# Attention softmax and null value handled another way, and the scores moved back in each TensorE slot

## The chip, the cores and the metric

The kernel runs on one core of one Trainium2 chip. Its time is the device time of one execution in microseconds (us). TensorE (PE in the profile), VectorE (DVE), ScalarE (ACT) and GpSimd (POOL) each work through their own list of instructions in order, SyncE (SP) issues most of the transfers, and the lists meet only at semaphores.

## The reference

Four layers are added to x in turn, x of shape 2 x 1024 x 256. Two are causal attention with 16 heads of 64 and one key and value that all heads share; two are mixtures of 8 experts of width 128 (best two of eight, plus a shared expert of width 256). Cut to what the change touches, for each of the two attention layers:

```python
xn = ln(x, g)
q = heads(xn @ Wq)                       # 16 heads of 64 (first layer: l2-normalised, scaled)
k, v = split(xn @ Wkv)                   # one k and one v of 64 for all heads
k = concat([null_kv[0], k]); v = concat([null_kv[1], v])     # a null key and value ahead
sim = q @ k.T * scale + concat([null_bias, bias])
sim = where(causal & mask, sim, -inf)
out = softmax(sim) @ v                   # the null column has a weight too
y = ln(out.reshape(b, n, 16 * 64) @ Wout, g_out)
x = x + y
```

So the output of a head is (sum over keys of p times v, plus p_null times v_null) divided by (sum of p, plus p_null).

## The kernel before

All operands of the large matmuls are split into a float16 high part and a float16 low part, and `three` (lines 1084 to 1088) adds high x high, high x low and low x high in PSUM. After a head of some 90 us (position bias table, weights) come the two attention layers and then the two expert layers.

**Steps, units, slots.** Attention is cut into 512 steps. Step n is one head of one 128-row tile of one batch item. Four heads (h = n % 4) make a unit, 8 units (4 head groups x 2 items) are one tile T, and there are 8 tiles a layer. With causality tile t (0 to 7) has nk = t + 1 key blocks of 128 columns, so a step is 128 to 1024 columns wide. This text calls the eight tiles of the first layer T0 to T7 and those of the second T8 to T15 (as wide as T0 to T7). Every engine runs the same loop over slots n, with m, k = divmod(n, 4), and does in slot n what is due for several steps at different distances:

- PE: the scores of step n + 3 (L1203, L1204), then by k the projection by Wo (k = 0, L1214 to L1219), the projection of q of unit m + 3 (k = 1), the transposes of q (k = 3, L1227); then the transposes of the probabilities of step n into `tp` (L1312), the products of step n - 1 with v (`pv`, L1152) and the small things of `small()` (at k = 2 the transposes of the normalised output, L1300).
- DVE: score plus bias and its row maximum for step n + 2 (L880), at k = 3 the low part of q (L908), then the low part of the probabilities `p_lo` (L964), and small things.
- ACT: exp of step n + 1 (L630), at k = 3 the high part of q (`q_b`, L651, and its copy into `q_a`, L655), then the high part of the probabilities `p_hi` (L722).
- POOL: null column, normalisation, the splitting of the weights.

**Groups.** The probabilities are transposed block by block into one of two PSUM banks `tp`, copied to `p_hi` and subtracted to `p_lo` by groups of up to four blocks of one head. A step of 1 to 4 blocks is one group, one of 5 to 8 blocks is two. Buffers: two `tp`, four `p_hi`, four `p_lo`, two `probs`, two `biased`, two score banks `sc`, one bank `op` for the four heads of a unit. PSUM bank `aux` serves everything else, one user after the other (`take`); in tiles of at most four key blocks the unused half of a score bank helps out (`free_banks`).

**Row sums, null column, output.** The exp (L630) also writes the sum of its row (`accum_out`, `rows`). At k = 3 POOL forms `d_null` (L506), ACT `p_null` (L731), POOL `denom` (L511) and `o_null` = p_null x v_null for the four heads (L514). At k = 1 of the next unit DVE adds `op` and `o_null` into `o_raw` (L859), which frees `op` for the next unit, and takes the reciprocal (L862); POOL multiplies into `o_n` (L479), PE transposes, ACT and DVE split, and PE projects by Wo at k = 0.

## Time and profile before

| what | value |
|---|---|
| median of 3 runs | 1735.9 us (1734.8 to 1736.44) |
| the profiled execution | 1732.54 us |
| span of its instructions | 1730.6 us |
| mean granted TensorE clock | 0.972 |
| attention, from the first to the last start of L880 | 89.58 to 1353.2 us |
| busy share of the span | PE 85%, DVE 81%, ACT 70%, POOL 43% |

The span runs from the first to the last instruction; the profiled execution's own time has some 2 us around it. Busy time of an engine in a stretch is the time in which at least one of its instructions was under way, and an idle time is put down to what released it.

### The profile page before, as it was taken

The numbers are of one execution on the slowest core, as the hardware profiler recorded it, in microseconds if no ns is written. First come the engines' busy times: TensorE is split into PE (matmuls) and PEld (weight loads), VectorE is DVE, ScalarE is ACT, GpSimd is POOL, SyncE is SP. The second block draws the span as 40 slices with busy tenths as digits, with TensorE's granted clock in tenths as the row PEclk, the third lists the DMA queues.
The fourth block names the chain that finished last, engine by engine and source line by source line (L and its number), as shares of the span: only waits on it lengthen the run. The fifth ranks groups of instructions, "written<-read, shape, count | busy, mean of one in ns | idle before, by whom it ended". The sixth has DMA issues, their size and how long they took to land.

```text
span 1730.6 us, 46424 instructions
## 1 busy us (share of the span) xinstructions
PE 1470.3 (85%) x16377; PEld 1081.0 (62%) x16377; DVE 1410.4 (81%) x3651; ACT 1210.2 (70%) x3064; POOL 751.0 (43%) x1412
## 2 busy tenths in 40 slices
PE   2467778888889999977888888999999799999998
PEld 1245556666677777766666666777777555555555
DVE  4557778888889999977788888999999687777777
ACT  1268778888889899978888888989999432332232
POOL 5557776443434334366554232223222365522222
PEclk9779999999999999989999999999999899999999
DMA  4002122111211223012121212221223000000000
GB/s 138 7 24 62 51 62 75 57 62 69 75 58 67 87 99 99 33 44 62 51 81 52 85 63 75 75 81 62 82 99 99 1 25 19 1 1 1 13 13 25
DMA packets 50440, 96.70 MB, mean 56 GB/s; under 512 B 3332, under 2 KB 27028, under 8 KB 50212
## 3 DMA queue, kind: packets, MB, share of 16 engines
q1 hardware_dynamic: 45504, 90.27, 15.8%
q10 hardware_dynamic: 4708, 3.45, 0.7%
q8 instruction: 135, 2.21, 0.5%
q14 instruction: 93, 0.76, 0.1%
HBM read 91.54 MB, written 2.17 MB: 54 GB/s over the span
## 4 chain that ended last, share of the span: by engine, by line
PE 42%; DVE 21%; ACT 14%; issue 11%; POOL 3%; DMA 1%; DVEq 0%; ACTq 0%; SPq 0%; POOLq 0%
PE tp L1312 7%; DVE p_lo L964 7%; ACT p_hi L722 6%; DVE biased L880 5%; PE sc L1203 3%; PE sc L1086 3%; PE sc L1087 3%; PE sc L1088 3%; ACT q_b L651 3%; PE sc L1204 3%; ACT probs L630 3%; PE op L1086 2%; PE aux L1086 2%; PE tp L1086 2%; PE aux L1088 2%
## 5 line engine op out<-in xcount | busy, mean ns | idle before, releaser
L964 DVE TENSOR_TENSOR p_lo<-tp,p_hi 128x512 f16<-128x512 f32 (+3 forms) x768 | 416.6, 554 | 121.3 <-ACT p_hi L722 114.3
L880 DVE CUSTOM_DVE_ANT_0 biased<-sc,bias,neg_null 128x256 f32<-128x256 f32 (+7 forms) x512 | 411.0, 803 | 2.7 <-issue 0.8
L630 ACT ACTIVATE probs<-biased,neg_max 128x256 f32<-128x256 f32 (+7 forms) x512 | 395.7, 773 | 14.2 <-DVE neg_max L880 12.7
L1312 PE MATMUL tp<-ident,probs 128*128 128x128 f32 x2304 | 388.7, 278 | 17.7 <-DVE p_lo L964 15.5
L722 ACT ACTIVATE p_hi<-tp 128x512 f16<-128x512 f32 (+3 forms) x768 | 368.9, 491 | 43.6 <-PE tp L1312 33.5
L1086 PE MATMUL op<-v_s,p_hi 128*128 128x64 f16 x2304 | 284.9, 194 | 54.4 <-DVE p_lo L964 35.9
L1203 PE MATMUL sc<-k_a,q_a 128*128 128x512 f16 (+3 forms) x768 | 254.2, 331 | 66.2 <-DVE neg_max L880 59.3
L1312 PEld LDWEIGHTS tp<-ident,probs 128*128 128x128 f32 x2304 | 267.9, 142 | 52.9 <-issue 37.9
L1088 PE MATMUL op<-v_s,p_lo 128*128 128x64 f16 x2304 | 284.0, 194 | 0.0
L1087 PE MATMUL op<-v_s,p_hi 128*128 128x64 f16 x2304 | 283.9, 194 | 0.0
L1086 PEld LDWEIGHTS op<-v_s,p_hi 128*128 128x128 f16 x2304 | 216.0, 99 | 85.5 <-DVE p_lo L964 62.1
L1204 PE MATMUL sc<-k_b,q_b 128*128 128x512 f16 (+3 forms) x768 | 241.9, 329 | 0.0
L1087 PEld LDWEIGHTS op<-v_s,p_hi 128*128 128x128 f16 x2304 | 210.3, 98 | 7.5
L1088 PEld LDWEIGHTS op<-v_s,p_lo 128*128 128x128 f16 x2304 | 210.5, 98 | 0.0
L570 POOL TENSOR_TENSOR p_lo<-probs,p_hi 128x512 f16<-128x512 f32 x80 | 92.5, 1156 | 213.7 <-ACT p_hi L755 213.3
L511 POOL TENSOR_TENSOR denom<-rows,p_null 128x4 f32<-128x4 f32 x128 | 25.6, 200 | 324.9 <-ACT p_null L731 324.9
L1203 PEld LDWEIGHTS sc<-k_a,q_a 128*128 128x128 f16 x768 | 75.1, 98 | 129.5 <-DVE neg_max L880 88.5
L755 ACT ACTIVATE p_hi<-probs 128x512 f16<-128x512 f32 x80 | 50.4, 630 | 145.5 <-DVE probs L1068 145.5
L479 POOL TENSOR_TENSOR o_n<-o_raw,r_den 128x256 f32<-128x256 f32 x128 | 78.4, 613 | 146.7 <-DVE o_raw L859 145.7
L908 DVE TENSOR_TENSOR q_a<-aux,q_b 64x256 f16<-64x256 f32 x256 | 108.1, 422 | 27.6 <-ACT q_b L651 19.9
L1063 DVE SCALAR_TENSOR_TENSOR biased<-sc,biased 128x512 f32<-128x512 f32 x80 | 55.2, 689 | 69.2 <-ACT biased L751 69.2
L651 ACT ACTIVATE q_b<-aux 64x256 f16<-64x256 f32 x256 | 96.5, 377 | 20.4 <-PE aux L1227 14.4
(257 smaller groups left out, 3611.4 us busy)
## 6 DMA issues: line engine op xcount, KB each, us to landing
bias<-rel_table SPq DMA_DIRECT2D x4, 2048.0 KB, 8.5
bias<-in_fside_16xSxS SPq DMA_DIRECT2D x4, 2048.0 KB, 7.9
bias<-rel_table SPq DMA_DIRECT2D x4, 1792.0 KB, 7.9
bias<-in_fside_16xSxS SPq DMA_DIRECT2D x4, 1792.0 KB, 7.1
bias<-rel_table SPq DMA_DIRECT2D x4, 1536.0 KB, 7.3
bias<-in_fside_16xSxS SPq DMA_DIRECT2D x4, 1536.0 KB, 6.7
bias<-rel_table SPq DMA_DIRECT2D x4, 1280.0 KB, 5.6
bias<-in_fside_16xSxS SPq DMA_DIRECT2D x4, 1280.0 KB, 6.3
```

The lines of the kernel that those rows point to most:

```text
L630: ac.activation(probs[:, i % 2, 0:w], biased[:, i % 2, 0:w], ACT.Exp, bias=neg_max[:, u % 2, i % HU:i % HU + 1], scale=-1.0, accum_out=row ...
L651: ac.activation(heads(q_b[0:DH, u % 2, :], e), first[e * DH:(e + 1) * DH, 0:UW].rearrange("p (c q) -> p c q", q=P), ACT.Copy)\
L722: ac.activation(p_hi[:, gi % 4, 0:nb * P], tp[gi % 2][:, 0:nb * P], ACT.Copy)\
L880: ve.tensor_tensor_reduce(out=biased[:, i % 2, 0:w], in0=sc[i % 2][:, 0:w], in1=bias[:, g % 2, i % HU, 0:w], scale=-1.0, scalar=neg_null[: ...
L908: ve.tensor_tensor(heads(q_a[DH:P, u % 2, :], e), first[e * DH:(e + 1) * DH, 0:UW].rearrange("p (c q) -> p c q", q=P), heads(q_b[0:DH, u % ...
L964: ve.tensor_tensor(p_lo[:, gi % 4, 0:nb * P], tp[gi % 2][:, 0:nb * P], p_hi[:, gi % 4, 0:nb * P], ALU.subtract).then_inc(s["p_lo"], 1)
L1086: te.matmul(out_, l_hi, r_hi, start=first, stop=False)
L1087: te.matmul(out_, l_hi, r_lo, start=False, stop=False)
L1088: return te.matmul(out_, l_lo, r_hi, start=False, stop=last)
L1203: te.matmul(o_, q_a[:, u % 2, cols], k_a[layer][:, bt, c0:c0 + cw], start=True, stop=False)
L1204: last = te.matmul(o_, q_b[:, u % 2, cols], k_b[layer][:, bt, c0:c0 + cw], start=False, stop=True)
L1312: last = te.transpose(tp[gi % 2][:, jj * P:(jj + 1) * P], probs[:, n % 2, (j0 + jj) * P:(j0 + jj + 1) * P], ident[:, :])
```

## The change

1. **Ones column.** `v_s` gets a 65th column, 1 in the high part and 0 in the low part, so that the product with v gives the row sum in `op` too (65 columns a head). The exp loses `accum_out`, and `rows` goes.
2. **Groups across heads.** The blocks of the four heads of a unit are counted through, and four in a row make a group, whatever head they are of. Each group is full. `p_hi` and `p_lo` are made when a group is complete, in the slot of the head that completes it.
3. **q copy on DVE.** The copy of `q_b` into `q_a` (64 x 512 float16, SBUF to SBUF) goes from ACT to DVE, ahead of the two L908.
4. **Null value at the projection.** `o_null`, `o_raw` and POOL's `o_n` go. DVE adds `p_null` to the row sums in `op`, takes the reciprocal and multiplies `op` by it into `o_n`. POOL keeps p_null / denom in `pn` (at k = 2), PE transposes `pn` once all 16 heads of a tile and item are there (k = 3), ACT copies it to `pn_t`, and the projection by Wo gets one more float32 matmul, `pn_t` x `nv_w`, for the last head group. `nv_w` = v_null x Wo per head is made once a layer (slot 12) by 24 matmuls.
5. **Order.** In each PE slot the scores of step n + 3 stand behind the first part of the transposes of step n, and so also behind the projections and the transposes of q.
6. Around it: a few memsets and copies in the head, `wt_n`, `wg_n`, `cond_n` inside `bias`, the load of the second bias waits for their use, `d_null` at k = 2, `p_null` doubled.

```diff
@@ class Plan
+        for u in range(self.steps // HU):
+            nk = self.tile(u * HU) + 1
+            blocks = [(u * HU + h, j) for h in range(HU) for j in range(nk)]
+            for b0 in range(0, len(blocks), 4):
+                group = blocks[b0:b0 + 4]
...
+                self.finished[group[-1][0]].append(len(self.groups))
+                self.groups.append(group)
@@ POOL
-                if k == 1 and 1 <= m <= NU:
+                if k == 2 and 1 <= m <= NU:
                     u = m - 1
-                    pool.wait_ge(s["o_raw"], u + 1)
...
-                    gp.tensor_tensor(o_n[:, :, :], o_raw[:, :, :],
-                                     r_den[:, :].unsqueeze(2).to_broadcast([P, HU, DH]), ALU.mult)\
-                        .then_inc(s["o_n"], 1)
...
+                    gp.tensor_tensor(pn[:, T % 2, bt, hg * HU:(hg + 1) * HU], p_null[:, u % 2, :], r_den[:, :], ALU.mult)\
+                        .then_inc(s["pn"], 1)
...
-                    gp.tensor_tensor(denom[:, :], rows[:, u % 2, :], p_null[:, :], ALU.add).then_inc(s["denom"], 1)
...
-                    gp.tensor_tensor(o_null[:, :, :], null_v[:, :].unsqueeze(1).to_broadcast([P, HU, DH]),
-                                     p_null[:, :].unsqueeze(2).to_broadcast([P, HU, DH]), ALU.mult)\
-                        .then_inc(s["o_null"], 1)
@@ ACT
                     ac.activation(probs[:, i % 2, 0:w], biased[:, i % 2, 0:w], ACT.Exp,
-                                  bias=neg_max[:, u % 2, i % HU:i % HU + 1], scale=-1.0,
-                                  accum_out=rows[:, u % 2, i % HU:i % HU + 1]).then_inc(s["probs"], 1)
+                                  bias=neg_max[:, u % 2, i % HU:i % HU + 1], scale=-1.0).then_inc(s["probs"], 1)
...
-                    act.wait_ge(s["q_hi"], 2 * (u + 1))
-                    ac.activation(q_a[0:DH, u % 2, :], q_b[0:DH, u % 2, :], ACT.Copy).then_inc(s["q_dup"], 1)
...
+                    if k == 3 and 0 <= m - 1 < NU and (m - 1) % UNITS >= UNITS - B:
...
+                        ac.activation(pn_t[:, u % B, :], turned(pn_ps) if u < U0 else pn_ps, ACT.Copy)\
+                            .then_inc(s["pn_s"], 1)
...
-                        act.wait_ge(s["pt"], gi + 1)
+                        act.wait_ge(s["pt"], plan.group_end[gi])
...
+                        ac.activation(p_hi[:, gi % 4, :], tp[gi % 2][:, :], ACT.Copy).then_inc(s["p_hi"], 1)
@@ DVE
-                    dve.wait_ge(s["o_null"], u + 1)
+                    dve.wait_ge(s["p_null"], u + 1)
                     dve.wait_ge(s["pv"], plan.groups_done(n - 2))
-                    ve.tensor_tensor(o_raw[:, :, :], op[:, 0:UW].rearrange("p (h d) -> p h d", h=HU),
-                                     o_null[:, :, :], ALU.add).then_inc(s["o_raw"], 1)
-                    dve.wait_ge(s["denom"], u + 1)
+                    link(ve.tensor_tensor(denom[:, :], o_ps[:, :, DH], p_null[:, u % 2, :], ALU.add))
+                    if u >= 1:
+                        dve.wait_ge(s["pn"], u)
                     ve.reciprocal(r_den[:, :], denom[:, :]).then_inc(s["r_den"], 1)
+                    dve.wait_ge(s["r_den"], u + 1)
+                    if u >= 1:
+                        dve.wait_ge(s["ot"], u)
+                    ve.tensor_tensor(o_n[:, :, :], o_ps[:, :, 0:DH],
+                                     r_den[:, :].unsqueeze(2).to_broadcast([P, HU, DH]), ALU.mult).then_inc(s["o_n"], 1)
...
                     dve.wait_ge(s["q_hi"], 2 * (u + 1))
+                    ve.tensor_copy(q_a[0:DH, u % 2, :], q_b[0:DH, u % 2, :]).then_inc(s["q_dup"], 1)
@@ PE, pv
+                    last = three(op[:, h * (DH + 1):(h + 1) * (DH + 1)], p_hi[:, gi % 4, cols], p_lo[:, gi % 4, cols],
+                                 v_hi, v_lo, j == 0, j == nk - 1)
@@ PE, slot n (the scores stood here, ahead of everything)
-                i = n + 3
-                if 0 <= i < N:
...
-                    last.then_inc(s["scores"], 1)
                 if k == 0 and 0 <= m - 2 < NU:
...
+                    if hg == HG - 1:
+                        pe.wait_ge(s["pn_s"], u // UNITS * B + u % B + 1)
...
+                        last = te.matmul(first[:, 0:D], pn_t[:, u % B, :], nv_w[:, :], start=False, stop=True)
...
+                    if k == 3 and 0 <= m - 1 < NU and (m - 1) % UNITS >= UNITS - B:
+                        u = m - 1
+                        T, bt = u // UNITS, u % B
+                        take(True, (s["pn_s"], T * B + bt + 1))
+                        pe.wait_ge(s["pn"], u + 1)
+                        te.transpose(second[0:H, 0:P], pn[:, T % 2, bt, :], ident[:, :]).then_inc(s["pn_t"], 1)
...
+                for j in range(max(1, len(parts), len(before))):
+                    if j < len(parts):
                         pe.wait_ge(s["probs"], n + 1)
+                        for _, jb in parts[j]:
+                            gi, at_ = plan.group_of[n, jb]
+                            if at_ == 0 and gi >= 2:
+                                pe.wait_ge(s["p_lo"], gi - 1)
+                            last = te.transpose(tp[gi % 2][:, at_ * P:(at_ + 1) * P],
+                                                probs[:, n % 2, jb * P:(jb + 1) * P], ident[:, :])
+                            if at_ == 3 or jb == nk - 1:
+                                last.then_inc(s["pt"], 1)
+                    if j == 0 and 0 <= n + 3 < N:
+                        scores(n + 3)
                     if j < len(before):
                         pv(before[j])
                     if j == 0:
```

## Rows read from the trace of the kernel before

**Rows 1.** The page: busy us of each engine, share of the span, instructions.

```profile
PE 1470.3 (85%) x16377; PEld 1081.0 (62%) x16377; DVE 1410.4 (81%) x3651; ACT 1210.2 (70%) x3064; POOL 751.0 (43%) x1412
```

**Rows 2.** Stretch, us, busy us by engine: T0-T3, T4-T7, T8-T11, T12-T15; T7.

```profile
89.58:356.79 267.21, 201.43 (x2330) 152.33 (x2331) 204.09 (x669) 213.85 (x674) 170.55 (x340) 0.95 0.18 54
356.79:741.11 384.32, 352.60 (x4632) 272.96 (x4629) 349.62 (x801) 338.70 (x797) 157.69 (x310) 1.00 0.21 72
741.11:988.60 247.49, 202.65 (x2427) 157.94 (x2425) 197.12 (x640) 204.98 (x632) 132.11 (x281) 0.97 0.21 61
988.60:1353.20 364.60, 341.11 (x4552) 267.28 (x4551) 331.11 (x748) 324.83 (x741) 95.76 (x204) 1.00 0.22 79
...
638.43:741.11 102.68, 99.16 (x1348) 78.06 (x1347) 98.66 (x197) 93.63 (x194) 42.84 (x85) 1.00 0.22 75
```

**Rows 3.** Who waited for whom, whole span: total us, times, longest.

```profile
DVE p_lo L964 <- ACT p_hi L722: 114.3, 275, 2.0
...
DVE q_a L908 <- ACT q_b L651: 19.9, 44, 1.5
...
ACT p_hi L722 <- PE tp L1312: 33.5, 105, 0.6
...
PE sc L1203 <- DVE neg_max L880: 59.3, 119, 2.6
...
PE op L1086 <- DVE o_raw L859: 15.8, 16, 1.9
```

**Rows 4.** Groups by line and shape: count, busy us, mean ns, idle before.

```profile
L964 DVE TENSOR_TENSOR p_lo<-tp,p_hi 128x512 f16<-128x512 f32 x384 | 262.9, 689 | 70.1 <-ACT p_hi L722 66.1
...
L630 ACT ACTIVATION_READ_ACCUMULATOR probs<-biased,neg_max 128x1 f32 x512 | 100.3, 196 | 0.0
...
L655 ACT ACTIVATE q_a<-q_b 64x512 f16<-64x512 f16 x128 | 80.6, 630 | 4.0
...
L964 DVE TENSOR_TENSOR p_lo<-tp,p_hi 128x128 f16<-128x128 f32 x128 | 36.4, 285 | 17.4 <-ACT p_hi L722 16.0
...
L987 DVE BATCH_NORM_AGGREGATE y_mv<-y_st 128x2 f32<-128x6 f32 x32 | 5.8, 182 | 1.1
```

**Rows 5.** Timeline of ACT, then DVE, in T1: start us, length us.

```profile
151.27 0.39 ACT L722 ACTIVATE p_hi<-tp 128x256 f16<-128x256 f32 x1
151.53 0.52 ACT L630 ACTIVATE probs<-biased,neg_max 128x256 f32<-128x256 f32 x1
151.93 0.21 ACT L630 ACTIVATION_READ_ACCUMULATOR probs<-biased,neg_max 128x1 f32 x1
152.02 0.39 ACT L722 ACTIVATE p_hi<-tp 128x256 f16<-128x256 f32 x1
...
149.94 0.42 DVE L964 TENSOR_TENSOR p_lo<-tp,p_hi 128x256 f16<-128x256 f32 x1 [0.44 <-ACT p_hi L722]
150.28 0.15 DVE L947 SCALAR_TENSOR_TENSOR neg_null<-sc,null_b 128x4 f32<-128x4 f32 x1
```

**Rows 6.** Single lines: duration ns min/median/max.

```profile
L901 DVE TENSOR_SCALAR xn<-x,mv,rstd x32: 400/409/819, 59.7 to 1217.9; 128x256 f32<-128x256 f32 x32
...
L827 DVE COPY p_hi<-null_k x2: 180/180/181, 41.1 to 41.5; 128x64 f32<-128x64 f32 x2
...
L840 DVE COPY cond_t<-op x1: 140/140/140, 48.8 to 48.8; 64x2 f32<-64x2 f32 x1
...
L1105 PE MATMUL sc<-bias,moe_w x32: 379/379/793, 38.0 to 46.9; 128*128 128x256 f32 x32
```

**Rows 7.** Groups by line and shape: the same L901, with its mean.

```profile
L901 DVE TENSOR_SCALAR xn<-x,mv,rstd 128x256 f32<-128x256 f32 x32 | 16.6, 557 | 8.5 <-POOL rstd L523 8.4
```

**Rows 8.** Timeline of T7, of PE: start us, length us, how many (x).

```profile
685.79 0.27 PE L1086 MATMUL aux<-wq,moe_w 128*128 128x256 f16 x1
...
686.45 0.60 PE L1312 MATMUL tp<-ident,probs 128*128 128x128 f32 x4
...
686.88 0.19 PE L1086 MATMUL op<-v_s,p_hi 128*128 128x64 f16 x1
...
```

More of the change, by code:

```diff
@@ L78, in unit @@
         return n // HU
-    def of(self, n):
-        return range(self.first_group[n], self.first_group[n + 1])
     def at(self, n):
-        return list(self.of(n)) if 0 <= n < self.steps else []
+        return self.finished[n] if 0 <= n < self.steps else []
     def groups_done(self, n):
-        return self.first_group[n + 1]
+        return max((gi for i in range(n // HU * HU, n + 1) for gi in self.finished[i]), default=-1) + 1
 def model(nc, a, out):
@@ L257, in model @@
                     x_st x_rs xn xt xt_hi xt_lo xr_hi xr_lo kv kv_act kv_r kv_d kv_v k_dup kt k_hi k_lo
-                    d_null p_null denom r_den o_null o_raw o_n ot ot_hi ot_lo y y_s y_acc
+                    d_null p_null r_den pn pn_t pn_s nv_w nv_o o_n ot ot_hi ot_lo y y_s y_acc
                     y_st y_rs y_n x_new""")
@@ L386, in _ @@
             load_bias(sp, 0)
+            sp.wait_ge(setup["mt"], 1)
             load_bias(sp, 1)
@@ L422, in _ @@
             gp.memset(ones64[:, :], 1.0).then_inc(setup["ones"], 1)
+            gp.memset(nv_f, 0.0).then_inc(setup["nv0"], 1)
+            for i in range(2):
+                for hl in range(2):
+                    gp.memset(v_s[i][:, :, hl, DH:DH + 1], 1.0 - hl).then_inc(setup["v1"], 1)
             for e in range(E):
@@ L832, in _ @@
                              kn_a[0:DH, :], ALU.subtract).then_inc(setup["nkb"], 1)
+            dve.wait_ge(setup["nv0"], 1)
+            for e in range(2):
+                half = slice(e * DH, (e + 1) * DH)
+                last = ve.tensor_copy(nv_f[half, e::18], nv_c[half, 0:1].to_broadcast([DH, INNER // P]))
+            link(last)
+            nv_f3 = nv_f.rearrange("p (c h) -> p c h", h=H)
+            link(ve.tensor_copy(nv_s[:, 0, :, :], nv_f3))
+            ve.tensor_tensor(nv_s[:, 1, :, :], nv_f3, nv_s[:, 0, :, :], ALU.subtract).then_inc(setup["nvs"], 1)
             dve.wait_ge(setup["mt"], 1)
@@ new lines, in small @@
+                    if n in NULL_AT:
+                        layer = NULL_AT.index(n)
+                        take(True, (s["nv_o"], layer + 1))
+                        pe.wait_ge(setup["nvs"], 1)
+                        pe.wait_ge(job_done, job_end[3 * layer + 2])
+                        for c in range(INNER // P):
+                            last = three(second[0:H, 0:D], nv_s[:, 0, c, :], nv_s[:, 1, c, :],
+                                         wo[layer][:, 0, c, :], wo[layer][:, 1, c, :], c == 0, c == INNER // P - 1)
+                        last.then_inc(s["nv_w"], 1)
@@ new lines, in _, with scores @@
+                nk = plan.tile(n) + 1 if 0 <= n < N else 0
+                def scores(i):
+                    layer, t, u = plan.layer(i), plan.tile(i), plan.unit(i)
+                    bt, h = u % B, i % HU
+                    if i == 0:
+                        pe.wait_ge(setup["penalty"], 2)
+                        pe.wait_ge(setup["mm"], 3)
+                    if h == 0:
+                        pe.wait_ge(s["q_dup"], u + 1)
+                        pe.wait_ge(s["q_lo"], 2 * (u + 1))
+                        if u % UNITS == 0:
+                            pe.wait_ge(s["k_lo"], u // UNITS + 1)
+                    if i >= 2:
+                        pe.wait_ge(s["biased"], i - 1)
+                    cols = slice(h * P, (h + 1) * P)
+                    w = P * (t + 1)
+                    if w > 512:
+                        release(i % 2)
+                        free[i % 2] = ()
+                    for c0 in range(0, w, 512):
+                        cw = min(512, w - c0)
+                        o_ = sc[i % 2][:, c0:c0 + cw]
+                        te.matmul(o_, q_a[:, u % 2, cols], k_a[layer][:, bt, c0:c0 + cw], start=True, stop=False)
+                        last = te.matmul(o_, q_b[:, u % 2, cols], k_b[layer][:, bt, c0:c0 + cw],
+                                         start=False, stop=True)
+                    last.then_inc(s["scores"], 1)
```

175 lines of the change are left out of this document (81 added, 94 removed).

## The prediction, made blind

> **What bounds the kernel now.** I read the page first, then the busy time by stretch, then the list of waits, then the groups by shape, and the timeline last, for how instructions follow on one another. The page alone misleads: PE is busy 85%, DVE 81%, ACT 70% [rows 1], but that is a mean over a head, attention and the expert layers, and the change touches attention alone, 1263.6 us of the span. There no single engine is the bound. In the narrow tiles (T0 to T3, T8 to T11) DVE, ACT and PE are each busy 75 to 83% of the time, in the wide ones (T4 to T7, T12 to T15) 88 to 94%, and in T7 PE has 99.2, DVE 98.7 and ACT 93.6 of 102.7 us [rows 2]. PE's figure flatters it in narrow tiles, since matmuls overlap, but in T7 its issue is really full: a projection of six matmuls takes from 685.79 to 686.45, four transposes from there to 686.88, and the products follow at once [rows 8]. So a wide tile is set by DVE and PE together, and a narrow one by the handovers between three engines that work in order.
>
> I count in DVE's time, because DVE is in every handover and full in the wide tiles. Its busy time in attention is 204.1 + 349.6 + 197.1 + 331.1 = 1081.9 us, its idle time 181.7: 63.1, 34.7, 50.4 and 33.5 in the four stretches [rows 2]. Of this 114.3 us is `p_lo` waiting for `p_hi` on ACT, 19.9 is q's low part waiting for its high part; `p_hi` itself waited only 33.5 for the transposes, so mostly ACT was late because it was busy [rows 3].
>
> **The change, part by part, in DVE time.** One thing first. Lengths are not spacings. The read of the accumulator behind each exp is 0.196 us long [rows 4], but the next ACT instruction starts 0.09 after it; a 0.39 us copy is followed after 0.26; and on DVE a 0.42 us instruction after 0.34 [rows 5]. Back to back, ACT saves some 0.12 and DVE some 0.08 of each length. I take spacings.
>
> *ACT is relieved.* Ones column: 512 reads x 0.09 = 46 us (not the 100.3 that the group shows). The q copy: 128 x (0.63 - 0.12) = 65 [rows 4]. Groups: before, a unit of four heads has 4 groups up to four key blocks and 8 above, after it has nk. Over a layer that is 8 x (16 + 32) = 384 against 8 x 36 = 288, so 192 fewer over both layers, and the columns stay the same. A `p_hi` of 256 columns takes 0.26 of spacing, of which I put 0.05 down as fixed: 10 us. Together ACT loses 121 of its 1082 us in attention [rows 2, 5].
>
> *DVE is loaded.* `p_lo`: 285 ns for 128 columns and 689 for 512 give 135 ns per block and 150 fixed [rows 4], 0.07 in spacing; 192 x 0.07 = -14 us. `o_raw` becomes `o_n`, the same shape and also out of PSUM: nothing. `denom`: four columns, as L947's 0.15 us [rows 5], 0.07 in spacing. It and the reciprocal now each hand over to the next instruction of DVE itself, which loses the 0.08 overlap and the 0.03 that a chained L987 idles (1.1 us over 32) [rows 4]: 2 x 0.11. The q copy is an operation that the trace does not show at this size. Below: 0.14, a copy of 2 columns. Above: 0.69, the 128 x 512 subtraction. A copy of 64 float32 columns takes 0.18, so 0.65 ns a column [rows 6]; 512 at that rate are 0.47, and at twice the rate, as half the bytes, 0.30. I take 0.30, in spacing 0.22. To it I add 0.10 for hold-ups: L901, a one-input instruction from SBUF to SBUF as the copy is, has a median of 409 ns, a maximum of 819 and a mean of 557 [rows 6, 7]. So 0.32 + 0.07 + 0.22 = 0.61 us a unit, x 128 = +78. Net DVE work: +64 us, 16 in each stretch.
>
> The Trainium skill (VectorE: DVE Perf Modes, the errata section) prices such a copy at 58 + 512/4 cycles at 0.96 GHz, 0.19 us; by it the sum would be 14 us lower. No row here has a float16 copy out of SBUF that could confirm it.
>
> *The waits.* With ACT 11% lighter, `p_hi` comes sooner. In T0 to T2 and T8 to T10 it also comes less often (1 to 3 times a unit instead of 4). And the transposes no longer stand behind scores that wait for the row maximum of two steps before; PE idled 59.3 us there [rows 3]. The transposes are never later for it: before they stood behind everything that they stand behind now, and the scores too. The scores come later by the projections and transposes, at most some 1.7 us, but are wanted by DVE only in the next slot, and a slot is 2.1 us on average in T0 to T3 (267.2/128) and 3.2 in T7. So DVE's idle time should about halve: I take 32, 16, 28 and 16 us off the four stretches (little from T7, where only 4.0 is left), 92 of 181.7. With the added work that gives -16, 0, -12 and 0: **-28 us**. The wide tiles end about even because two effects cancel; T7 alone should be slower, by 1 to 5 us, and the narrowest tiles gain most.
>
> *PE is loaded.* 32 float32 matmuls of 256 columns at 0.38 [rows 6] are 12 us; 32 transposes at 0.11, 48 matmuls for `nv_w` at 0.11 (six of 256 columns in 0.66 us [rows 8]) and one column more in 6912 products (0.4 ns each, estimated from 0.11 us for 256) are 3.5, 5 and 3. Of these 24 us I count a quarter, 6: DVE is now the fuller engine in wide tiles and PE idles in narrow ones. If PE stayed the fuller one all 24 would show. The products of a unit's first group wait until `op` is read; that was one DVE instruction (15.8 us of PE idle [rows 3]) and is three, 0.6 us more, but transposes and scores now stand ahead of it, and in T0 to T2 its place moves on a slot or more. POOL loses 128 x two 256-column multiplies; it is at 43% [rows 1] and releases nobody on the path now: nothing. `d_null` comes a slot earlier, nothing. The head gets some five small DVE instructions at 0.15 to 0.2, partly in the way: +1. The expert layers: nothing.
>
> **Sum.** -28 + 6 + 1 = -21 us against the profiled execution's 1732.5, so 1711.5. That execution lies 3.4 below the median of the runs, so 1715 in their terms; I say 1714.
>
> **Rivals.** *A, the q copy is dear (slower).* Work on DVE is paid in full where DVE is full. The sum is zero when a unit costs DVE not 0.61 but 0.61 + 21/128 = 0.77 us, that is when the copy with its hold-ups takes 0.48 instead of 0.32. With 0.47 for the copy (no gain from float16) and half of L901's worst excess (0.41) on top it is 0.60: 128 x 0.28 = +36, **1750 us**. For it: the spread of L901. Against it: at k = 3 POOL has less to do than before. The Trainium skill (SBUF — State Buffer, Who interferes with whom) states a rule for this: a DVE copy from SBUF to SBUF that uses the second port pair and a POOL instruction exclude each other for their whole length. L901's 400 and 819 ns agree with it. 0.16.
>
> *B, the idle time nearly goes.* If lifting ACT and moving the transposes leaves DVE idle only 50 us (4% of the time, as T7 has now), the sum falls by 40: **1674 us**. For it: in narrow tiles all four slots of a unit have a wait for `p_hi` now and most lose it. Against it: the waits for PE on q, x and k stay. 0.16.
>
> *C, `aux` at k = 3.* In wide tiles the transpose of `pn` uses `aux` right after q's transposes, so PE must wait inside the slot until DVE has read q, ahead of its second part of transposes. 8 wide tiles x 2 units x about 1 us (copy and two L908, less what PE does meanwhile) = +16: **1730 us**. 0.12.
>
> *D, the order of waits is what holds it*, ACT was not: idle time falls by 50, not 92, work is added, +42: **1756 us**. Against it: the two waits on ACT are 134 of the 181.7. 0.08.
>
> **How the numbers follow.** My case has 0.48 and its own range is 1698 to 1730. With A to D the range reaches from B's 1674 to near A's 1750; cutting 1 in 10 at each side gives 1677 to 1745. About 0.2% (3.5 us) is what a measurement of this kernel can tell from no change, so faster is below 1732.4: my case nearly whole, B and two thirds of C, 0.72; within 0.2%, the top of my case and the rest of C, 0.09; slower, A, D and the tail of C, 0.19.
>
> **What would show it.** In the profile after: no accumulator reads on ACT, 576 `p_hi` and 576 `p_lo`, all of 512 columns; ACT's busy time in attention down by some 120; DVE's up by some 65 and its idle time near 90, with `p_lo` waiting for `p_hi` 114.3 down to about 45; T0 to T3 near 251 us and T8 to T11 near 235, T7 at 104 to 108. The copy's row decides A: 0.30 us with a mean under 0.4 is mine. I would be wrong if DVE in the wide tiles were held by PE after all (then all 24 us of PE's extras show), or if idle time in narrow tiles came from PE's in-order waits for `aux`, which the change does not lift.

## The result, and the profile after

The changed kernel takes 1847.8 us (median of 4 runs, 1846.9 to 1856.6) against 1736.2 for the kernel before beside it: ratio 1.065, interval 1.062 to 1.069. It is 112 us slower; 1714 was forecast. One of the four executions of e4 below had a granted clock of 0.65 and took 2216 us; it is left out of e4's times.

The page of the changed kernel: busy us of each engine.

```profile
PE 1512.1 (82%) x16521; PEld 1116.1 (60%) x16521; DVE 1474.3 (80%) x3719; ACT 1089.0 (59%) x2266; POOL 602.8 (33%) x1161
```

Against [rows 1] ACT has lost 121 us and POOL 148, DVE has gained 64 and PE 42. The busy times of ACT and DVE came out almost as forecast, and the time did not follow them. The same windows as in [rows 2], of the changed kernel (T0-T3, T4-T7, T8-T11, T12-T15, T7); the last columns are granted clock, DMA share and GB/s.

```profile
90.13:369.27 279.14, 210.10 (x2366) 157.22 (x2367) 218.71 (x685) 180.51 (x473) 135.23 (x278) 0.93 0.16 50
369.27:796.53 427.26, 365.18 (x4657) 287.65 (x4656) 367.59 (x817) 311.12 (x598) 119.99 (x247) 0.98 0.19 66
796.53:1060.23 263.70, 209.32 (x2474) 161.75 (x2472) 208.53 (x655) 174.01 (x432) 94.89 (x216) 0.94 0.20 56
1060.23:1465.00 404.77, 351.90 (x4579) 277.59 (x4576) 349.09 (x762) 296.09 (x543) 59.16 (x140) 1.00 0.20 71
680.78:796.53 115.75, 103.15 (x1363) 81.59 (x1362) 103.80 (x213) 86.57 (x157) 33.55 (x70) 1.00 0.20 66
```

Attention went from 1263.6 to 1374.9 us, and all four stretches are longer: by 11.9, 42.9, 16.2 and 40.2 us. DVE is busy 1143.9 us there (+62) and idle 231 (it was 181.7, and some 90 was forecast). In T7 no engine is full any more: of 115.8 us PE works 103.2, DVE 103.8, ACT 86.6. In the wide tiles every engine has become less full: the change made waits. PE's granted clock (the third number from the end) is a little lower too, 0.98 for 1.00 in T4 to T7 and 0.94 for 0.97 in T8 to T11; no run separates what that adds. Who waited for whom in the changed kernel:

```profile
PE op L1120 <- DVE p_lo L998: 82.0, 79, 2.3
...
DVE p_lo L998 <- ACT p_hi L743: 77.7, 134, 2.0
...
ACT probs L639 <- PE tp L1372: 68.2, 93, 1.7
ACT p_hi L743 <- PE tp L1372: 67.9, 136, 1.5
...
ACT probs L639 <- DVE neg_max L914: 56.3, 70, 1.6
...
PE aux L1238 <- DVE ot_lo L989: 38.2, 41, 1.5
...
DVE neg_null L982 <- PE sc L1302: 34.2, 42, 3.6
...
PE aux L1120 <- DVE q_a L943: 26.0, 44, 1.2
...
DVE denom L888 <- PE op L1122: 21.8, 42, 1.2
...
PE aux L1319 <- DVE q_a L943: 19.4, 16, 1.9
```

The waits have moved to PE. DVE's wait for ACT's `p_hi` fell by 37 us, from 114.3 [rows 3] to 77.7 (about 45 was forecast). But DVE now waits 56 us for PE, for the product of the null column (`neg_null`) and for the products with v (`denom`); before, the first was not there and the second, then `o_raw`'s, was under 1 us. ACT waits 136 us for PE's transposes of the probabilities (68.2 + 67.9, before 33.5 [rows 3]), and 56 for DVE's row maximum, where it was

```profile
ACT probs L630 <- DVE neg_max L880: 12.7, 32, 1.2
```

PE, which issues in order, stands longer in waits of its own: 82.0 us for `p_lo` ahead of the products with v, where it was 35.9, and in three for `aux`, of which L1319 is the new transpose of `pn`.

### The profile page after: what moved, and what is told of

Same layout as the page of the kernel before. It is cut to its first block, busy times and chain, and to the rows that moved or that the text cites. A ratio compares the mean times of both kernels' runs of the same rounds, so it can differ in the third digit from the quotient of the medians.

```text
span 1846.3 us, 45581 instructions
## 1 busy us (share of the span) xinstructions
PE 1512.1 (82%) x16521; PEld 1116.1 (60%) x16521; DVE 1474.3 (80%) x3719; ACT 1089.0 (59%) x2266; POOL 602.8 (33%) x1161
## 4 chain that ended last, share of the span: by engine, by line
PE 46%; DVE 30%; issue 11%; ACT 9%; POOL 2%; DMA 1%; DVEq 0%; ACTq 0%; SPq 0%; POOLq 0%
DVE biased L914 7%; PE tp L1372 7%; DVE p_lo L998 6%; DVE q_a L943 4%; PE sc L1120 4%; PE sc L1121 3%; PE sc L1122 3%; ACT p_hi L743 3%; PE aux L1120 3%; PE sc L1353 3%; PE sc L1354 3%; PE op L1120 2%; PE aux L1122 2%; PE aux L1121 2%; ACT q_b L659 2%
## 5 line engine op out<-in xcount | busy, mean ns | idle before, releaser
L639 ACT ACTIVATE probs<-biased,neg_max 128x256 f32<-128x256 f32 (+7 forms) x512 | 394.9, 771 | 126.6 <-PE tp L1372 68.2
L998 DVE TENSOR_TENSOR p_lo<-tp,p_hi 128x512 f16<-128x512 f32 x576 | 392.0, 689 | 83.9 <-ACT p_hi L743 77.7
L1372 PE MATMUL tp<-ident,probs 128*128 128x128 f32 x2304 | 397.9, 282 | 24.7 <-DVE p_lo L998 22.6
L743 ACT ACTIVATE p_hi<-tp 128x512 f16<-128x512 f32 x576 | 342.5, 596 | 75.5 <-PE tp L1372 67.9
L1120 PE MATMUL op<-v_s,p_hi 128*128 128x65 f16 x2304 | 275.5, 194 | 87.4 <-DVE p_lo L998 82.0
L1120 PEld LDWEIGHTS op<-v_s,p_hi 128*128 128x128 f16 x2304 | 219.3, 97 | 147.1 <-DVE p_lo L998 67.7
L1121 PE MATMUL op<-v_s,p_hi 128*128 128x65 f16 x2304 | 276.6, 197 | 0.0
L1122 PE MATMUL op<-v_s,p_lo 128*128 128x65 f16 x2304 | 274.0, 193 | 0.0
L1121 PEld LDWEIGHTS op<-v_s,p_hi 128*128 128x128 f16 x2304 | 218.4, 98 | 16.0 <-issue 0.8
L1122 PEld LDWEIGHTS op<-v_s,p_lo 128*128 128x128 f16 x2304 | 219.8, 100 | 0.0
L549 POOL TENSOR_TENSOR y_acc<-y_acc,y_s 128x256 f32<-128x256 f32 x96 | 69.8, 727 | 352.8 <-ACT y_s L652 352.8
L1086 DVE SCALAR_TENSOR_TENSOR x<-tp,comb,x 128x256 f32<-128x256 f32 x256 | 106.0, 475 | 0.1
```

The lines of the kernel that those rows point to most:

```text
L639: ac.activation(probs[:, i % 2, 0:w], biased[:, i % 2, 0:w], ACT.Exp, bias=neg_max[:, u % 2, i % HU:i % HU + 1], scale=-1.0).then_inc(s["p ...
L743: ac.activation(p_hi[:, gi % 4, :], tp[gi % 2][:, :], ACT.Copy).then_inc(s["p_hi"], 1)
L998: ve.tensor_tensor(p_lo[:, gi % 4, :], tp[gi % 2][:, :], p_hi[:, gi % 4, :], ALU.subtract)\
L1120: te.matmul(out_, l_hi, r_hi, start=first, stop=False)
L1121: te.matmul(out_, l_hi, r_lo, start=False, stop=False)
L1122: return te.matmul(out_, l_lo, r_hi, start=False, stop=last)
```

## The experiments

All times are medians with the ratio to the kernel before, run beside it on the same chip (its median was 1735.8 to 1736.4 us each time). Five edits were taken out of the changed kernel or put alone into the kernel before. An edit shown as a diff is cut to its main lines. Five results lie outside every range that was expected for them: e3, e5, e7, e10 and e13.

### The order

e1 is the changed kernel with the scores back at the head of the slot, e2 the kernel before with the scores moved. The edit of e1:

```diff
+                if 0 <= n + 3 < N:
+                    scores(n + 3)
                 if k == 0 and 0 <= m - 2 < NU:
...
-                    if j == 0 and 0 <= n + 3 < N:
-                        scores(n + 3)
```

> The changed kernel with the scores of step n + 3 first in the PE slot again, all else as changed. Theory O (the order costs the time): scores between the two parts of the transposes put 0.86 us of a wide tile between the last use of one half of a step and the next, and leave the handovers of aux at the head of the slot with no work in front of them; without it 1710 to 1740 us, and DVE's wait of p_lo for p_hi in the tile of T7's width falls from 9.5 us to about 2. Rival P (the other parts cost it: groups across heads, three DVE instructions instead of one on op, pn in aux): stays above 1820.

> The kernel before with the order alone: scores of step n + 3 behind the first group of transposes. Theory O: 1810 to 1860 us, with the wide tiles paying 8 to 13 us each. Rival P: within 15 us of 1736. A third, that only both together are slow (the loop is long only with the three DVE instructions on op and the copy on DVE in it): 1736 to 1770.

e1 took 1835.6 us (1.0571, 1.0553 to 1.0589), e2 1752.1 (1.0096, 1.008 to 1.0111). So the order costs 16 us by itself and 12 within the change. It is not one effect. The difference of e2 to the kernel before is -11.1, +18.4, -10.6 and +22.2 us in the four stretches: every narrow tile gains 1 to 4.6 us, every wide one loses 1.8 to 7.4. The first theory for both runs, that the order is what costs the time, is out.

PE's largest new wait in e2 is one for `aux`, ahead of the transposes of q (k = 3), which want the bank while DVE is still reading it for `ot_lo`. Over the run it went from 5.6 us (20 times) to

```profile
PE aux L1200 <- DVE ot_lo L954: 47.0, 60, 1.6
```

In the kernel before the four score matmuls of a wide tile (0.9 us) ran while DVE read. But this wait does not fall where the tiles lose. It is 8.2 us in T4, which loses 1.8, and 2.4 us in T15, which loses 7.4. And of the 40.6 us that the wide tiles lose, 30.9 lie in one slot in four, from DVE's `biased` in the slot with k = 0 to the next one. There DVE's wait for the `p_hi` of a step's second part went from 3.9 to 31.3 us (summed out of the two timelines). This is that slot in T7 of e2, first PE, then ACT, then DVE:

```profile
712.87 0.63 PE L1312 MATMUL tp<-ident,probs 128*128 128x128 f32 x4
713.33 0.38 PE L1298 MATMUL sc<-k_a,q_a 128*128 128x512 f16 x1
...
714.75 0.63 PE L1312 MATMUL tp<-ident,probs 128*128 128x128 f32 x4
...
715.42 0.60 ACT L722 ACTIVATE p_hi<-tp 128x512 f16<-128x512 f32 x1 [0.90 <-PE tp L1312]
...
716.05 0.69 DVE L964 TENSOR_TENSOR p_lo<-tp,p_hi 128x512 f16<-128x512 f32 x1 [0.74 <-ACT p_hi L722]
```

and the same place in T7 of the kernel before, PE and DVE:

```profile
693.62 0.38 PE L1203 MATMUL sc<-k_a,q_a 128*128 128x512 f16 x1
...
696.20 0.63 PE L1312 MATMUL tp<-ident,probs 128*128 128x128 f32 x4
...
697.22 0.64 PE L1312 MATMUL tp<-ident,probs 128*128 128x128 f32 x4
...
699.09 0.68 DVE L964 TENSOR_TENSOR p_lo<-tp,p_hi 128x512 f16<-128x512 f32 x1
```

The first four transposes need a `tp` bank, and in both kernels they mostly start some 0.15 us after DVE's `p_lo` has given it back. Before the move PE did the scores while it waited for that. Behind the move the scores stand between the two parts, so the second part comes 1.88 us after the first and not 1.02 (over all wide tiles 1.72 and 1.08), and ACT and DVE wait for it. In this slot the products of the null column stand there as well. So this is what the traces show the wide tiles to lose; no run takes the one wait without the other. In the changed kernel the order does the same: against e1 its wide tiles lose 30 us, 28 of them in that slot, and its narrow ones gain 11.

In narrow tiles the scores are short, a step has one part only, and the wait of the scores on `neg_max` was the great one (59.3 us over the run [rows 3], 9.2 of them in T4 to T7). If so, moving the scores in narrow tiles alone must keep the gain without the loss. e12:

```diff
+                behind = plan.tile(max(n, 0)) < TILES // 2
+                if not behind and n + 3 < N:
+                    scores(n + 3)
...
+                    if j == 0 and behind and 0 <= n + 3 < N:
+                        scores(n + 3)
```

> The kernel before with the scores behind the first transposes only in tiles of up to four key blocks, first in the wide ones. By the tiles of the two kernels that I have: the narrow ones gained 4.0, 1.0, 1.7, 4.5 and 1.7, 1.7, 2.7, 4.6 us, the wide ones lost 1.8 to 7.4 each; so 1710 to 1716 us, faster than both kernels. If the gain of a narrow tile is only time that the next wide one returns: 1730 to 1740.

It took 1713.5 us, 0.9868 (0.9853 to 0.9882): 1.3% under the kernel before and 7% under the changed one, and within the bounds. Its tiles T0 to T3 are e2's within 0.3 us (52.6, 62.5, 68.8, 72.6 us), T4 to T7 those of before (90.3, 92.8, 98.6, 102.7).

### Groups across heads

e5 is e1 with groups that end with their head, as before; e8 the kernel before with groups across heads alone. The edit of e5:

```diff
-            blocks = [(u * HU + h, j) for h in range(HU) for j in range(nk)]
-            for b0 in range(0, len(blocks), 4):
-                group = blocks[b0:b0 + 4]
+            per_head = [[(u * HU + h, j) for j in range(b0, min(b0 + 4, nk))]
+                        for h in range(HU) for b0 in range(0, nk, 4)]
+            for group in per_head:
...
```

> The changed kernel, scores first, and the groups of one head each again (768 groups of 128 to 512 columns). Theory G (the full groups come late and in bursts, in the slots that already carry the extra work of the unit): most of the 96 us by which the scores-first kernel is over the kernel before come back, in the tiles whose groups straddle heads (T1, T5, T6, T9, T13, T14 lost 5 to 11 us each); total 1760 to 1785 us; T7 and T15, where the groups are the same either way, stay at 111 and 102. Rival N (the null value, with pn in aux, and the three instructions on op cost it): within 15 us of 1835.

> The kernel before with the groups across heads alone. Theory G: 1775 to 1820 us, T1, T5, T6, T9, T13 and T14 each 5 to 10 us slower than before, T3 and T7 as before. Rival N: 1715 to 1740, 24 us of busy time saved on ACT and DVE.

e5 took 1799.3 us (1.0369, 1.0353 to 1.0384), 36 less than e1; e8 1782.1 (1.0268, 1.0253 to 1.0283), 46 more than the kernel before. This edit costs the most but for the null value below, and I had counted it as a gain of 10 us on ACT and 14 on DVE. The lengths of the tiles say what it is (us, from the tile's first `biased` to the next tile's, out of DVE's timeline):

```
T            0     1     2     3     4     5     6     7     8     9    10    11    12    13    14    15
before    56.3  63.4  70.5  77.0  90.3  92.8  98.6 102.7  55.3  57.2  63.2  71.7  86.3  89.1  93.5  95.7
e8        61.4  69.3  71.4  78.0  89.3  97.6 106.6 104.0  58.6  64.9  65.8  72.6  83.3  92.1 101.4  97.0
```

T3, T7, T11 and T15 have 4 or 8 key blocks, so there the groups are the same in both kernels: +0.8 to +1.3 us. In T6 and T14, with 7 blocks, a group holds the last blocks of one head and the first of the next: +8.0 and +7.9. In T0 and T1 a group is full only with the fourth or second head: +5.1 and +5.9 (T8 and T9: +3.3 and +7.7). Only T4 and T12, with 5 blocks, where 8 groups become 5, gain 1.0 and 3.0. In e8's waits:

```profile
PE op L1092 <- DVE p_lo L970: 79.8, 91, 2.6
...
PE tp L1321 <- DVE p_lo L970: 32.8, 79, 1.1
```

The first was 35.9 us and the last 15.5. I read them so: a group that waits for its last head keeps its `tp` bank and its `p_lo` a slot longer, so products, and the transposes that want the bank, come late. DVE's wait for `p_hi`, which was to fall, rose from 114.3 to 129.3 (237 times), and a new one came, 18.5 us for the product of the null column. The cost and the tiles in which it lies are measured; this way from the group to the cost is read from the waits, and no run tests it by itself.

### The q copy, the 65th column, the row sum

e3 is e1 with the q copy back on ACT, e10 the kernel before with it on DVE, e16 is e12 with it on DVE; e4 pads `v_s` from 65 to 66 columns in e1; e14 is the kernel before with 65 columns (the 65th is not used). The edit of e10 and e16, which e3 takes back:

```diff
+                    ve.tensor_copy(q_a[0:DH, u % 2, :], q_b[0:DH, u % 2, :]).then_inc(s["q_dup"], 1)
...
-                    ac.activation(q_a[0:DH, u % 2, :], q_b[0:DH, u % 2, :], ACT.Copy).then_inc(s["q_dup"], 1)
```

> Scores first as in the first kernel of this call, and the copy of q_b into q_a back on ACT. DVE is relieved by 128 x (0.285 - 0.07) = 28 us, ACT loaded by 65. If DVE sets the pace of the wide tiles in this order: 10 to 20 us faster than the scores-first kernel, most of it in the wide tiles; if ACT's load costs as much in the narrow ones: within 5 us of it.

> The kernel before with the q copy moved from ACT to DVE alone. ACT 65 us lighter, DVE 128 x 0.22 to 0.32 = 28 to 41 us heavier. By my forecast's prices about 15 us faster (49 us less idle time, 28 to 41 more work). Theory D (DVE's own work comes through nearly in full everywhere, ACT's relief does not): 20 to 40 us slower than before.

> The kernel before with the scores behind the first transposes in narrow tiles only (1713.5 us) and the q copy on DVE. In the kernel before the copy's move changed nothing (ratio 1.000): T1 lost 2.3 us, the other tiles gained 0 to 1.4. Here within 4 us of 1713.5. If the narrow tiles, now tighter, feel DVE's extra work: 1720 to 1728.

> Scores first, and v_s padded to 66 columns of float16 so that each row starts on 4 bytes (65 are still read). The products stand 31.0 ns apart in the changed kernel against 29.1 before. If the odd start costs that: back to 29.5, 6912 x 1.5 ns = 10 us of PE, some 5 us of time; if it is the 65th column: no change within 0.2%.

> The kernel before with products of 65 columns (a ones column that nothing reads), all else as before. 5 to 13 us slower than before, most of it in the wide tiles, if the spacing of the products is what counts; within 3 us if TensorE has that much to spare.

e3 1829.0 us (1.0537, 1.052 to 1.0554), 7 below e1; e10 1736.1 (1.000, 0.999 to 1.0009), no change; e16 1716.2 (0.9894, 0.9877 to 0.991), 3 more than e12. In e10 the copy takes 64 us of busy time in attention from ACT and gives DVE 28, and it never gains; the 3 us between e16 and e12 are hardly more than their intervals. e4 took 1835.3 to 1840.8 us (1.0592, 1.0569 to 1.0615), no better than e1, e14 1735.7 (1.0003, 0.9993 to 1.0013): the column is free on the chip, padded or not.

e9 is the kernel before without `accum_out`; it leaves out the row sums, and the denominator has a constant in their place.

```diff
...
-                                  bias=neg_max[:, u % 2, i % HU:i % HU + 1], scale=-1.0,
-                                  accum_out=rows[:, u % 2, i % HU:i % HU + 1]).then_inc(s["probs"], 1)
+                                  bias=neg_max[:, u % 2, i % HU:i % HU + 1], scale=-1.0).then_inc(s["probs"], 1)
```

> The kernel before without the row sum of the exp (no accumulator read on ACT; the sums are left out, a constant stands in their place, so the output is scaled wrongly). ACT is 46 us lighter by spacing and nothing else changes. My forecast priced the relief of ACT through the wait of p_lo for p_hi: 121 us of relief for 92 of idle time; by it 30 to 40 us faster than before. Theory L (the wait is set by the order of the queues and by two-deep buffers, not by how full ACT is): under 10 us faster.

It took 1729.6 us (0.9959, 0.9944 to 0.9974). Taking 46 us of spacing from ACT, with nothing given to anyone, brings 7. That is what relief of ACT was worth here, and my forecast assumed several times as much. DVE's idle time in attention hardly moved, from 181.7 to 178.2 us. It did take up work of DVE's own: in e10 DVE works 28 us more there and idles 26 less.

### The null value at the projection

e11 is e5 with the q copy on ACT: ones column, normalisation on DVE and null value at the projection are all that is left of the change. e13 is e11 without `pn`, its transposes, `pn_t`, `nv_w` and the last matmul of the projection, and so leaves the null value's share out of the output; e15 is e13 with 64 columns and a constant denominator, so the row sums are left out too.

> The changed kernel, scores first, groups of one head, q copy on ACT: what is left is the ones column, the three instructions of DVE on op and the null value at the projection. Theory D: 25 to 40 us under the 1799 of the same kernel with the copy on DVE. If the copy's cost lies only in the wide tiles: 5 to 12 us under it.

> The kernel of ones column, normalisation on DVE and null value (scores first, groups of one head, q copy on ACT: 1791.5 us) without the null value: pn, its transposes, nv_w and the float32 matmuls are left out, so the output lacks v_null's share. If the null value at the projection costs it (its 16 waits of TensorE in aux are 20.0 us, 30 waits of ACT's y copy 29.6, the 48 matmuls of nv_w and their copy 7): 1745 to 1760. If it is the normalisation on DVE or the 65th column: 1775 to 1792.

> The same without the 65th column too: products of 64 columns, and the denominator a constant formed by an instruction of the same shape that still reads op. Null value and row sums are left out. 6912 products x 1.9 ns are 13 us of TensorE: 8 to 13 us under the kernel that leaves out the null value alone if TensorE sets the wide tiles, under 4 if not. What remains over 1730 is the price of the three instructions of DVE on op, 128 x 0.3 = 38 us of DVE at most.

e11 took 1791.5 us (1.032, 1.0305 to 1.0335), e13 1728.5 (0.9965, 0.9952 to 0.9978), e15 1728.5 (0.9963, 0.995 to 0.9977). So the sums by the 65th column and the three DVE instructions of the normalisation cost nothing that shows (1728.5 against e9's 1729.6; DVE works 27 us more in attention than in the kernel before and idles 32 less). `pn` with its product costs 63 us. Of the 24 us of PE time in my sum, which I counted at 6, 21 were for it. Slot by slot, attention is 57 us longer in e11, and 46 of these lie in the steps of each tile in which the last two units hand over their `pn` and are projected (the expectation of e17 puts 56 there, which is all of attention). Another 6.5 lie in the two slots, one a layer, behind which ACT waits for the 24 matmuls of `nv_w`. Two more runs split it: e17 is e11 without the product, e18 e11 with it in float16.

```diff
@@ e17
...
-                        last = te.matmul(first[:, 0:D], pn_t[:, u % B, :], nv_w[:, :], start=False, stop=True)
@@ e18
-        pn_t = sb("pn_t", [H, 2, P])
-        nv_w = sb("nv_w", [H, D])
+        pn_t = sb("pn_t", [H, 2, P], F16)
+        nv_w = sb("nv_w", [H, D], F16)
```

> e11_ones_null_only (ones column, normalisation and null value at the projection, groups per head, scores first, q copy on ACT) without the float32 product pn_t x nv_w at the end of the projection; the transposes of pn, their copies to pn_t and POOL's multiplies stay. It leaves out the null value's share of the output. The pair with and without all of it stands at 1791.5 and 1728.5 us, and 56 us of the 63 lie in two steps of each tile: those in which the last two units' pn is transposed and their output projected. Theory 'the product': two float32 passes with weight loads stand on PE between the projection and the next tile step's transposes, 0.72 us each time, 32 times, and ACT's copy of y waits for them; without it the time falls by 23 us to 1768 us (1760 to 1775), and the stretch between the last projection product and the next transposes shrinks from 0.8 to 0.1 us. Rival 'the hand-over of pn': the transposes of pn wait on DVE's reading of the q bank and hold the transposes behind them, 32 times 1 to 2 us; then it stays at 1785 us or above. Rival 'all of it is the product': ACT in its order is held at the copy of y, and with the product gone the rest is hidden; then it is below 1745 us.

> e11_ones_null_only with pn_t and nv_w held in float16, so the product is one float16 instruction instead of two float32 passes; it rounds the two factors of the null value's share to float16. Theory 'the product': the float16 product costs PE 0.11 us like the six ahead of it instead of 0.72, so the time falls to within 6 us of the run without the product: 1772 us (1762 to 1780). Rival 'the hand-over of pn': no more than 5 us below 1791.5. Rival 'the place of any product that waits for pn_s': float16 changes nothing, 1788 to 1793, while the run without the product falls.

e17 took 1765.6 us (1.0184, 1.016 to 1.0207), e18 1777.4 (1.0247, 1.0215 to 1.028). The product is 26 us of the 63 (32 times 0.81), and the float16 product 12, twice what was expected over e17. The other 37 us are not the hand-over of `pn` alone: e17 still makes `nv_w`, which e13 does not, and that is the 6.5 us again. So some 30 us are left for the hand-over (32 times 0.95). Neither rival explains it all; both are there. The product, in PE's timeline of T7 in e11:

```profile
666.34 0.27 PE L1124 MATMUL aux<-wo,ot_lo 128*128 128x256 f16 x1
666.54 0.69 PE L1260 MATMUL aux<-nv_w,pn_t 16*128 16x256 f32 x2
667.17 0.65 PE L1376 MATMUL tp<-ident,probs 128*128 128x128 f32 x4
```

and the same place in e17:

```profile
661.79 0.27 PE L1124 MATMUL aux<-wo,ot_lo 128*128 128x256 f16 x1
661.90 0.27 PE L1371 MATMUL tp<-ident,probs 128*128 128x128 f32 x1
```

From the last projection matmul to the next transposes it is 0.83 us in the one and 0.11 in the other. One matmul in the code is two instructions on PE ("x2"), and its 0.72 us stand in front of the transposes for which ACT waits. The hand-over, in e17's waits of PE:

```profile
PE aux L1345 <- DVE q_a L944: 20.0, 16, 1.9
...
PE sc L1122 <- ACT pn_t L728: 8.3, 11, 1.1
```

and in the rows of the tile `pn`:

```profile
L1345 PE MATMUL aux<-ident,pn x18: 274/277/370, 372.7 to 1395.0; 128*16 128x128 f32 x18
...
who waited for it (us, times):
  ACT pn_t L728: 6.1, 11
  PE sc L1345: 5.8, 5
```

These waits come to 20.0 + 8.3 + 5.8 = 34 us and e13 has none of them: PE waits inside the slot for DVE to leave the bank with q (20.0), for POOL's `pn` (5.8), and then for ACT to take `pn_t` out (8.3). Each time the transposes of `probs` stand behind. Would another place be cheaper? e6 is e1, and e7 is e5, with the transpose of `pn` at k = 2 in front of those of `o_n`, in the same bank.

```diff
+                        if last_hg:
+                            pe.wait_ge(s["pn"], u + 1)
+                            te.transpose(second[0:H, 3 * P:4 * P], pn[:, T % 2, bt, :], ident[:, :]).then_inc(s["pn_t"], 1)
                         pe.wait_ge(s["o_n"], u + 1)
```

> The changed kernel, scores first, with the transpose of pn at k = 2, in the same bank and the same turn as the transposes of the output, not at k = 3 behind q's. In the scores-first kernel TensorE waited 28.0 us for DVE's reading of q in front of that transpose, 16 times, and 6.0 for POOL. Rival N: 25 to 40 us faster than 1835.6. Theory G: under 10 us faster, since other waits take over.

> Both: groups of one head and pn at k = 2. What is left of the change is the ones column, the q copy on DVE, the output normalised on DVE and the null value at the projection. If they work as I costed them (ACT 110 us lighter, DVE 78 us heavier, PE 24 heavier): 1715 to 1745 us. If the waits of PE on q_a and op stay: 1750 to 1780.

e6 took 1831.3 us (1.0549, 1.0533 to 1.0565), 4 less than e1, e7 1804.8 (1.0401, 1.0384 to 1.0418), 6 more than e5. The wait for `q_a` was gone, and in its place e7 has

```profile
PE sc L1344 <- POOL pn L495: 18.3, 7, 3.4
...
PE aux L1344 <- POOL pn L495: 12.5, 9, 2.8
```

At k = 2 `pn` isn't ready when PE asks: the chain behind it (`denom`, reciprocal, POOL's multiply) has not ended. So the one place waits for the bank and the other for the data. The edit also makes DVE's `ot_lo` wait until ACT has taken `pn_t` out of the shared bank, 29.3 us (21 times) in e7, so e6 and e7 do not test the place alone.

### The account

Each line is the difference of two kernels above, in us.

```
row sum gone, ones column, normalisation on DVE   e13 - before    -7.3
hand-over of pn (some 30), nv_w (6.5)             e17 - e13      +37.0
float32 product in the projection                 e11 - e17      +26.0
q copy on DVE                                     e5 - e11        +7.7
groups across heads                               e1 - e5        +36.3
order                                             after - e1     +12.2
sum                                                             +111.9
```

Alone in the kernel before the last three come to 0, +46 and +16. Only the first is a gain, and it is the one that takes work away and adds no hand-over.

## Why the prediction was wrong

**The work was counted right.** ACT lost 121 us in attention (1082.3 to 961.7), as forecast. DVE gained 62, forecast 64. There are 576 `p_hi` and 576 `p_lo`. The copy's row in the changed kernel, min, median and max in ns:

```profile
L941 DVE COPY q_a<-q_b x128: 251/285/773, 85.8 to 1446.1; 64x512 f16<-64x512 f16 x128
```

The median of 0.285 us stands by my 0.30, and the mean of 0.356 is under the 0.4 that I had named. The 0.19 us that follow from the table of the Trainium skill (VectorE: DVE Perf Modes, the errata section) are below even the shortest copy here. The same section says that this row comes out too short and that the measured fixed part is some 150 cycles instead of 58. By that an estimate is 150 + 512/4 = 278 cycles at 0.96 GHz, 0.29 us, which agrees with the median.

**The step that failed is "So DVE's idle time should about halve".** I took idle time for a stock out of which relief of ACT is paid: 121 us lighter, 92 us back. e9 gives the rate: 46 us off ACT bring 7. The idle time in attention rose by 49 us, to 231: the wait for `p_hi` did fall by 37, but 56 us of waits for PE came in its place, and smaller ones. It hung on the order of hand-overs between engines that issue in order, which the new order, the groups, the hand-over of `pn` and its product lengthened. DVE's added work, booked at its full 64 us, was not the cost either: 28 us of it in e10 and 27 in e13 went into DVE's idle time. That is what I wrote for rival D ("the order of waits is what holds it", 1756), at 0.08. D was right in kind and short by 92 us, since it let the idle time fall by 50.

**"It also comes less often" was booked as a gain alone.** I saw fewer, fuller groups and that a first group's "place moves on a slot or more", and booked 24 us less work and part of the idle time. That a group is late by a head was the main thing: +36 to +46 us.

**"The transposes are never later for it".** It holds for the instructions that they stand behind, but not for time. In wide tiles the scores had filled PE's wait for a `tp` bank. With them moved, the first part of the transposes at k = 0 comes no earlier, since it still waits for the bank, and the second part comes 0.64 us later. The narrow tiles did gain as said (-22 us in e2 by itself); the wide ones, for which I had booked 32 us less of idle time, have 32 us more of it in e2 and lose 41. So the first of my two signs of being wrong was near: PE does hold the wide tiles, but by its order and not by the 24 us of its extra work. The second, waits for `aux` in narrow tiles, was not tested.

**"Of these 24 us I count a quarter" (PE loaded).** The product alone costs 26 us: I had 12 for it from L1105's 0.38 us, a length and not a spacing, then a quarter of that. I took one instruction of the row L1105 for a whole float32 matmul; here one is two instructions, with 0.72 us on PE. And it isn't hidden, since in that slot PE's issue is what ACT waits for. For the 65th column I had 3 us of PE time; it takes 13, but no time of the run (e14).

**Rival C was right in its place and its mechanism** (PE waits at k = 3 until DVE has read q: 16 times, up to 1.9 us), and near in size: 16 us for a wait that comes to 20. But it had one of the three waits that `pn` brings, and nothing for `nv_w` or the product. **A** did not decide: the copy on DVE costs 0 to 8 us. **B** ran the wrong way.

What stays open: what the `aux` wait at k = 3 adds to the loss of the wide tiles, how the late groups turn into time, why the q copy costs 8 us with the ones column, 3 with the narrow order and nothing by itself, and why the order costs 12 in the one and 16 in the other. The differences add up in the order in which I took them; in another order single lines would be some 10 us different.

## What to carry to other kernels

Idle time of an engine that is in every hand-over isn't a reserve out of which relief of its neighbour is paid: before booking that, take work off the neighbour by itself (e9) and see what it buys. It may still take up work of the engine's own (e10, e13). When a matmul group is moved in an in-order queue, look at both ends: what wait it filled where it stood, and who waits for what will stand behind it. Then compare tile by tile and slot by slot, since the wait that grew most (`aux`, 47 us) need not lie where the time is lost; the move pays only where nothing waits behind it (narrow tiles, e12). Batching across producers saves instructions and makes each consumer wait for the last producer; compare the two per stage, and the stages in which the batches stay the same are the control.

## What the runs showed of the hardware

**A copy on DVE that begins beside POOL's work ends behind it.** The timeline of the changed kernel, POOL and DVE:

```profile
587.23 0.72 POOL L563 TENSOR_TENSOR x<-x,y_acc 128x256 f32<-128x256 f32 x1
...
587.33 0.77 DVE L941 COPY q_a<-q_b 64x512 f16<-64x512 f16 x1
```

The copy starts at 587.33 while POOL works until 587.95, and ends at 588.10, so 0.15 us after it, instead of after 0.28. Of the 128 copies the 75 beside which POOL did nothing of over 0.25 us took 0.25 to 0.29 us; the 53 others have a mean of 0.46. This agrees with the rule of the Trainium skill (SBUF — State Buffer, Who interferes with whom) that rival A rested on; it costs 10 us of DVE's work over the run (53 times 0.19), which the forecast had as "hold-ups" (0.10 a copy, 13 us).

**Behind a stall at a hand-over PE ran at its lower clock.** Windows of e1 in T7, around the wait of 2.43 us for `q_a` before the transpose of `pn` at 700.45; the granted clock is the third number from the end:

```profile
697.00:700.00 3.00, 1.03 (x18) 0.89 (x16) 2.94 (x7) 1.36 (x3) 2.24 (x4) 1.00 0.00 0
700.00:702.00 2.00, 1.55 (x15) 1.49 (x16) 1.09 (x2) 0.54 (x2) 0.00 (x0) 0.53 0.00 0
702.00:704.00 2.00, 2.00 (x14) 1.02 (x12) 1.64 (x2) 1.45 (x3) 0.00 (x0) 0.61 0.03 8
704.00:706.00 2.00, 2.00 (x26) 1.42 (x25) 0.25 (x2) 0.61 (x2) 0.36 (x1) 1.00 0.00 0
```

PE had worked 1.03 of the 3 us before; then it ran near 1.2 GHz, the lower of its two levels, for some 3 us, with the 512-column scores following each other by 0.42 us instead of 0.22, and was back at full after them. So the stall took time of PE twice; how much of that lengthens the run, no run separates. The mean clock of the whole run shows little of it (0.964 in e1, 0.972 before).

**The 65th column costs spacing and no time.** Back to back, the products with v follow one another by 31.0 ns on average with 65 columns, padded or not, and by 29.1 with 64, a difference of 13 us over 6912 products, and e14 is 0.0003 from the kernel before.
